# Attention 0, block 0: who loads the next weights, behind what, and when inputs and statistics of the later blocks are prepared

## What is computed

```python
x = x + _L0_xattn_ref(_layernorm(x), ctx_4096, wq, wk, wv, wo)   # first attention
    q = (query @ wq).reshape(b, tq, 32, 128)
    k = (key @ wk).reshape(b, tk, 8, 128)
    v = (value @ wv).reshape(b, tk, 8, 128)
    scores = einsum('bqhd,bkhd->bhqk', q / sqrt(128), repeat(k, 4))
    out = einsum('bhqk,bkhd->bqhd', softmax(scores), repeat(v, 4))
    return out.reshape(b, tq, 4096) @ wo
x = x + _L0_ffn_ref(_layernorm(x), ...)
x = x + _L1_xattn_ref(...)
x = x + _L1_ffn_ref(...)
```

## Time and profile before

| | |
|---|---|
| median of 3 runs | 1686.51 us (1685.79 to 1689.08) |
| the profiled execution | 1685.48 us |
| its span, first to last instruction | 1683.7 us |
| PE busy | 1501.9 us, 89% of the span |
| VectorE busy | 1268.9 us, 75% |
| ACT busy | 855.8 us, 51% |
| mean granted TensorE clock | 0.963 of full speed |

### The profile page before, as it was taken

One profiled execution on the slowest core, in us unless ns is written; L12 is line 12 of the kernel. 1 busy time (PEld: TensorE's weight loads), 2 busy tenths in 40 slices (PEclk: granted clock), 3 DMA queues, 4 the chain that ended last, 5 costly groups with the idle time before them and its releaser, 6 DMA issues. The chain is left out here.

```text
span 1683.7 us, 29381 instructions
## 1 busy us (share of the span) xinstructions
PE 1501.9 (89%) x11227; PEld 794.4 (47%) x11227; DVE 1268.9 (75%) x2276; ACT 855.8 (51%) x1774; POOL 306.7 (18%) x271
## 2 busy tenths in 40 slices
PE   5888789999999999999999987699999988687686
PEld 3444454555455555555545543344444445344343
DVE  4676756667777677776777787789888885999777
ACT  3444434343443425344343342688888863888652
POOL 0212310001011111111010200001111002789620
PEclk9899989999999999999999998899999999999898
DMA  6445663131413231413323122223222350767402
GB/s 237 113 113 133 145 129 106 39 77 50 114 51 100 62 100 50 98 51 69 93 56 106 30 59 101 103 43 55 55 44 44 52 121 1 138 105 124 76 1 100
DMA packets 317143, 140.73 MB, mean 84 GB/s; under 512 B 265856, under 2 KB 290560, under 8 KB 316800
## 3 DMA queue, kind: packets, MB, share of 16 engines
q1 hardware_dynamic: 262848, 87.13, 24.1%
q10 hardware_dynamic: 54208, 52.44, 10.6%
HBM read 66.13 MB, written 11.53 MB: 46 GB/s over the span
## 5 line engine op out<-in xcount | busy, mean ns | idle before, releaser
L593 PE MATMUL pj<-XT,WQ 128*128 128x512 f16 x1536 | 339.8, 381 | 6.8 <-DVE WKV L289 6.4
L632 PE MATMUL xp<-WO,OT 128*128 128x512 f16 x1536 | 340.3, 381 | 4.3 <-DVE X L923 4.3
L632 PEld LDWEIGHTS xp<-WO,OT 128*128 128x128 f16 x1536 | 148.1, 98 | 187.5 <-issue 16.2
L593 PEld LDWEIGHTS pj<-XT,WQ 128*128 128x128 f16 x1536 | 148.6, 98 | 183.4 <-issue 9.9
L750 ACT ACTIVATE E<-E 128x512 f32<-128x512 f32 x64 | 40.2, 628 | 308.8 <-DVE E L900 308.8
L1164 PE MATMUL db<-W0T,XD 128*128 128x448 f16 x768 | 156.7, 362 | 16.0 <-DVE XD L1362 11.0
L923 DVE SCALAR_TENSOR_TENSOR X<-xp,X 128x512 f32<-128x512 f32 x128 | 88.3, 690 | 92.9 <-PE xp L632 91.9
L1182 PE MATMUL eb<-W1T,DT 128*128 128x512 f16 x672 | 149.1, 381 | 4.3 <-ACT eb L1269 4.3
L569 POOL TENSOR_TENSOR VW<-VW,XB 128x1024 f32<-128x1024 f32 x14 | 32.9, 2353 | 656.5 <-DVE VW L102 656.5
L860 DVE SCALAR_TENSOR_TENSOR QT<-pj,QT 128x512 f16<-128x512 f32 x128 | 88.1, 688 | 73.8 <-ACT QT L720 73.8
L1164 PEld LDWEIGHTS db<-W0T,XD 128*128 128x128 f16 x768 | 75.7, 100 | 94.7 <-DVE XD L1362 12.0
(11 more groups left out here) (239 smaller groups left out, 2482.2 us busy)
## 6 DMA issues: line engine op xcount, KB each, us to landing
W0T<-in_L_xattn_wo ACTq DMA_DIRECT2D x15, 1024.0 KB, 5.3
W0T<-in_L_xattn_wq ACTq DMA_DIRECT2D x14, 1024.0 KB, 5.8
X<-in_x SPq DMA_DIRECT2D x4, 1024.0 KB, 7.5
out<-X SPq DMA_DIRECT2D x8, 512.0 KB, 3.6
W0T<-in_L_xattn_wk ACTq DMA_DIRECT2D x14, 256.0 KB, 6.5
W0T<-in_L_xattn_wv ACTq DMA_DIRECT2D x14, 256.0 KB, 7.2
XB<-in_L_ffn_W ACTq DMA_DIRECT2D x28, 128.0 KB, 3.1
w0t<-XB ACTq DMA_DIRECT2D x7, 512.0 KB, 7.4
```

The lines of the kernel that those rows point to most:

```text
L593: last = pe.matmul(bank[:, :], w, src[:, b, k, tokens], start=n == 0, stop=n == 3 * KC - 1)
L632: last = pe.matmul(xp[i % 2][:, :], OT[:, a, j, i * P:(i + 1) * P], WO[:, b, j, :], start=n == 0, stop=n == 3 * REP - 1)
```

## The change

Four things are edited. SyncE now issues the load of the next weights (load_qkv), in each of slots 0 to 6, after a new wait for its own two PT transposes to land; ACT's load is taken out. The input pairs are prepared in slots 1 to 6 instead of 0 to 5 (on SyncE, ACT and, through the semaphores, GpSimd). PE's first unit waits for the split of WQ alone, and the key unit (u == 4) for the split of WKV, in every slot. The statistics of block 1 leave the place ahead of slot 0 and stand at the end of slot 0; those of blocks 2 and 3 move from slots 1 and 3 to slots 2 and 4.

```diff
             for cur in FIRST:
                 turn_probabilities(cur)
-                if cur.n < AHEAD_SLOTS:
-                    turn_inputs(cur.n)
+                sp.wait_ge(S["pt_done"], count(cur, 32, 32))
+                if cur.n < LAST:
+                    sp.wait_ge(S["qkv_lo"], 2 * cur.n + 4)
+                    load_qkv(sp, (cur.n + 2) % GROUPS)
+                if 1 <= cur.n <= AHEAD_SLOTS:
+                    turn_inputs(cur.n - 1)
...
                     if u == 0:
-                        pe.wait_ge(S["qkv_lo"], cur.w * 2 + 2)
+                        pe.wait_ge(S["qkv_lo"], cur.w * 2 + 1)
                         if turned:
                             pe.wait_ge(S["turned"], turned)
+                    if u == 4:
+                        pe.wait_ge(S["qkv_lo"], cur.w * 2 + 2)
...
             def first_slot(cur, nxt):
-                ahead = cur.n < AHEAD_SLOTS
+                ahead = 1 <= cur.n <= AHEAD_SLOTS
                 probabilities(cur, nxt)
                 high_o(cur)
-                if cur.n < LAST:
-                    act.wait_ge(S["qkv_lo"], 2 * cur.n + 4)
-                    load_qkv(act, (cur.n + 2) % GROUPS)
                 high(nxt, (2,))
                 if ahead:
-                    high_inputs(cur.n, 0)
+                    high_inputs(cur.n - 1, 0)
...
-                if cur.n in (1, 3):
-                    ln_stats_scalar(act, 0, (2 + cur.n // 2,))
+                if cur.n in (0, 2, 4):
+                    ln_stats_scalar(act, 0, (1 + cur.n // 2,))
...
-                stats = 2 + cur.n // 2 if cur.n in (1, 3) else None
+                stats = 1 + cur.n // 2 if cur.n in (0, 2, 4) else None
...
             low_q(dve, 1)
-            dve.wait_ge(S["x_ld"], 32)
-            ln_moments(dve, 0, 1)
             low(FIRST[0], 4)
-            ln_scales(dve, 0, 1)
             low(FIRST[0], 5)
             low_kv(dve, 1)
```

More of the change, by code:

```diff
@@ L759, in first_slot @@
             def first_slot(cur, nxt):
-                ahead = cur.n < AHEAD_SLOTS
+                ahead = 1 <= cur.n <= AHEAD_SLOTS
                 probabilities(cur, nxt)
                 high_o(cur)
-                if cur.n < LAST:
-                    act.wait_ge(S["qkv_lo"], 2 * cur.n + 4)
-                    load_qkv(act, (cur.n + 2) % GROUPS)
                 high(nxt, (2,))
                 if ahead:
-                    high_inputs(cur.n, 0)
+                    high_inputs(cur.n - 1, 0)
                 high(nxt, (3,))
                 if ahead:
-                    high_inputs(cur.n, 1)
+                    high_inputs(cur.n - 1, 1)
                 high(nxt, (4,))
@@ L840, in _ @@
             high_q(act, 1)
-            ln_stats_scalar(act, 0, (1,))
             high(FIRST[0], (4, 5))
```

## The result

The changed kernel takes 1642.52 us (median of 4 runs, 1641.09 to 1645.76) against 1686.65 us of the kernel before beside it: a ratio of 0.974, 95% interval 0.972 to 0.976. The profiled execution took 1641.23 us with a span of 1639.5 us, 44.2 us less than before, at a mean granted clock of 0.973 instead of 0.963.

A forecast was written before the change was run, and what follows sets the result against it. PE was the bound, delayed in slots 0 to 6 by a shared DMA. Savings of 4.9+7.6+31.5 = 44.0 us off the profiled 1685.48 gave 1641.5, or 1642.5 as the run median lies 1.03 us higher; range 1638 to 1648, chance 0.78.

The forecast's parts named there:

- opening: Before the first scores: first projection no longer waits for WKV's split, minus 1.2 us; block 1's statistics leave, minus 3.7 us.
- slot 0: First slot of block 0: no late PT, maxima still after low_kv(1); 31.2 us instead of 38.79.
- slots 1 to 6: Block 0: six slots of 29.80 us, plus 1.2 us in three after statistics and 0.3 us in all six; 184.2 us.
- behind block 0: The 24 later slots: a second wait at the key unit costs between minus 1 and plus 1 us, taken as 0.
- PT is late because of the load: First attention product, slots 0 to 6: the weight load delays PT's transposes; 5 us separate slots 6 and 7.
- Whole slots, not waits: Slots 0 to 6: PE's clock falls with the wait, so a slot loses more than its idle time.
- the terms for the statistics: VectorE in block 0: a slot after statistics costs 1.2 us more; slots 1, 3 and 5 pay it.
- GpSimd: Value unit, slots 1 to 6: input subtractions moved beside VectorE's low_o delay unit 3's split, 0.3 us per slot.
- SyncE's queue: Slots of block 0: after the load and input transposes, about 10 us remain before the next PT.
- rival 1: Block 0: wv taking 14 us makes low_kv 3.9 us late; 13 us given back, 1655 us; chance 0.09.
- margin of wq: ACT in block 0's slots: wq has landed by T+19.7, before ACT can split it at T+20.6 (T: first score matmul).
- rival 3: Block 0: late PT is not the load's doing, slots keep their length, only the opening counts; 1681.6 us; chance 0.03.

## Why the prediction was right

The prediction held: 1642.5 us forecast, 1642.52 us measured. Against the profiled execution, the terms:

| term | forecast, us | measured, us |
|---|---|---|
| opening (scores 44.33 to 38.49) | -4.9 | -5.84 |
| slot 0 (38.79 to 30.97) | -7.6 | -7.82 |
| slots 1 to 6 (215.72 to 184.47) | -31.5 | -31.25 |
| slot 7 (29.80 to 29.88) | 0 | +0.08 |
| behind block 0 | 0 | +0.63 |
| sum | -44.0 | -44.20 |

The agreement to 0.02 us is luck: the errors of the terms cancel, and the four runs lie 4.7 us apart. The steps:

- **PT is late because of the load.** Right, from the comparison of slots 6 and 7. Moving the load alone brings 39.1 us, moving all but the load brings nothing.
- **Whole slots, not waits.** Right: with the load alone 27.6 us of waits became 39.1 us, as PE's work itself took 13.6 us less.
- **Slot lengths.** 31.3 and 30.1 us were forecast, 31.36 and 30.13 us measured; the terms for the statistics (1.2 forecast, 1.23 measured) and GpSimd (0.3 forecast; 30.13 - 29.88 = 0.25 measured) hold.
- **The opening** was mis-sized by 0.9 us. The two terms are confirmed (1.17 us for the first wait, 3.85 us for the statistics); the rest is the first 48 projections, which took 11.98 us here and 13.04 us before. In kernels with this same opening that group took 11.98 to 13.48 us, so it is no gain of the change.
- **Later slots.** The 0.63 us lie within the bounds of 1 us either way. The kernel without the second wait needs 1356.1 us from the end of block 0 to the end of its span, this one 1355.7 us, so the second wait is not their cause. Of the 0.63 us, 0.47 lie in one slot, the fifth behind block 0 (29.59 us instead of 29.12), where PE waits 0.39 us for PT at 418.34; why PT is late there is open.
- **SyncE's queue.** Right: 9.8 to 12.8 us of margin for 10 forecast.

Four things in the working were wrong without touching the number. First, the prediction credited the new wait ("the load cannot be in flight with its own slot's PT"). The wait is not needed; issued behind both transposes, the load stays behind them by itself, and the wait only moves its first packet from 84.32 to 85.21 us in slot 1.

Second, rival 1 was priced on the wrong split. It let wv come late and hold up low_kv, 13 us in all. In the kernel with the later load, wq decides, through low_q and the output's accumulation, and PE loses 6.9 us per slot: 31.6 of the 41.6 us is idle time, the rest matmuls after it at a lower clock. The margin of wq, T+19.7 against T+20.6 in the prediction, was in its text and never entered the rival's price. The forecast stood because the margin held (1.8 us by the rows of slot 2). The load's place thus has an edge on both sides: between the PT transposes nearly everything is given back, behind the XT transposes too.

Third, rival 3 said that the opening alone would give 1681.6 us if PT stayed late. With PT left late the kernel took 1685.7 us: the opening did shrink, and the third set of statistics, the inputs in slot 6 and the waits and the lower clock in the slots took it back.

Fourth, the load was to start "about 3 us later", for which the prediction shows no row. It was issued at T+8.8 to T+10.7 before and at T+13.5 to T+14.7 after, 3.4 to 5.9 us later. The margin of wq held even so, as its forecast went by the new place (T+13.6) and not by the difference.

The rule "issue early, wait late" of the Trainium skill (page "DMA: Bandwidth & Descriptors", section "Rules for kernel authors"), by which the prediction's sum would have been 21 us worse, did not hold for this delay: the load had that much slack. It did hold for the 7.7 to 9.7 us more, where 41.6 us were lost.

## What to carry to other kernels

Compare a slot that lacks the suspected transfer with one that has it, and count whole slots, since the clock falls with the wait (1.00 without it here, 0.87 to 0.95 with it). A large load that is issued just ahead of a small transfer on the critical path, on its queue or on another, belongs behind it, and the time to its own first consumer bounds how far. As long as something ends late, savings ahead of it only lengthen the wait; take out the late one first, and then read which wait is left, as it may be a copy that fits into its engine's idle time.

## What the runs showed of the hardware

- A DMA transpose of the probabilities, issued ahead of a 1.5 MB load, lands in 2.8 us (median; 3.5 at most) even if the load is issued 0.04 us behind it, as the load's packets then start when the transpose's are through. Issued after the load it takes up to 4.5 us to issue and up to 7.0 us to land on the same queue, and up to 4.7 and 9.5 us with the load on ACT's queue: its packets start when wq's 1 MB is through or nearly so.
- The load hardly minds eight transposes behind it: wq lands in 5.5 us there and in 5.6 us in the later groups, which turn no inputs.
- After 4 to 6 us of idling, PE works on at a lower clock for a while: 12 output matmuls take 4.91 us in the kernel with the later load (four such tiles take 10.53 us without a wait), and the value unit 4.31 instead of 2.85 us in the one with the old load.
- The first 48 projections took 11.98, 12.12, 12.68, 13.19, 13.34, 13.40 and 13.48 us in kernels whose opening is the same up to there. A microsecond in the opening is thus no finding.
